# The last contraction chunk of a down projection: 96 rows packed into one full product and two half-array products

## The reference

```python
def _qlinear(x, q, scale, A, Bm):
    w = (q.astype(jnp.float32) - Q_ZERO) * (scale * Q_STEP)[:, None]
    y = jnp.einsum('bsh,oh->bso', x, w)
    return y + LR_SCALE * (x @ A @ Bm)
g = _qlinear(x, gate_q, gate_scale, gate_A, gate_B)
u = _qlinear(x, up_q, up_scale, up_A, up_B)
h = jax.nn.silu(g) * u
return _qlinear(h, down_q, down_scale, down_A, down_B)
...
x = x + _L0_ffn_ref(_L0_cond_ref(x, ...), ...)
x = x + _L1_ffn_ref(_L1_cond_ref(x, ...), L1_ffn_weight)
```

## Time and profile before

| What | Value |
|---|---|
| Median of 3 timed runs | 375.7 us (375.58 to 376.06) |
| Span of the profiled execution (no other time of it is given) | 375.1 us |
| TensorE busy, products | 365.7 us, 97% of the span |
| VectorE, ScalarE, GpSimd busy | 246.0, 190.5, 93.1 us |
| Mean granted TensorE clock | 0.995 of full speed |
| Share of TensorE in the chain that ended last | 82% |
| Products of the down stages (line 660) | 704, 24% of the chain |

### The profile page before, as it was taken

How to read it: one execution, slowest core, us unless ns; L and a number is a source line. 1 busy time by engine, 2 the same in 40 slices (tenths; PEclk the granted TensorE clock), 3 DMA queues, 4 the chain that set the end, 5 groups by cost and what they waited for, 6 DMA issues and landing times.

```text
span 375.1 us, 5791 instructions
## 1 busy us (share of the span) xinstructions
PE 365.7 (97%) x2208; PEld 302.5 (81%) x2208; DVE 246.0 (66%) x399; ACT 190.5 (51%) x345; POOL 93.1 (25%) x78
## 2 busy tenths in 40 slices
PE   8999999999999999999999999999999999998994
PEld 3777887899888888998888889998888899997331
DVE  3858999727476665263766652547889922588995
ACT  4557698403555554134565550235667511066972
POOL 2101432411133224111323232113223321142030
PEclk9899999999999999999999999999999999999999
DMA  7599676197320000142200000526000199977288
GB/s 218 178 228 367 193 264 215 54 336 154 53 44 0 0 0 3 22 64 42 43 0 2 2 0 2 83 36 160 0 3 1 48 287 268 197 163 180 92 174 276
DMA packets 82475, 41.72 MB, mean 111 GB/s; under 512 B 52416, under 2 KB 72784, under 8 KB 82320
## 3 DMA queue, kind: packets, MB, share of 16 engines
q1 hardware_dynamic: 69072, 37.70, 37.2%
q10 hardware_dynamic: 12624, 1.82, 3.1%
q0 software_dynamic: 752, 1.84, 2.5%
HBM read 26.55 MB, written 14.80 MB: 110 GB/s over the span
## 4 chain that ended last, share of the span: by engine, by line
PE 82%; DVE 7%; ACT 4%; DMA 2%; issue 2%; POOL 0%; DVEq 0%
PE ps L675 34%; PE ps L660 24%; PE ps L608 4%; PE ps L690 4%; PE ps L710 3%; PE ps L868 3%; DMA x_nat<-in_gate_q 2%; PE ps L568 2%; PE ps L666 2%; PE ps L712 2%; ACT mix L937 1%; PE ps L848 1%; DVE a_buf L1423 1%; PE ps L623 1%; ACT h_hi L979 1%
## 5 line engine op out<-in xcount | busy, mean ns | idle before, releaser
L1137 POOL TENSOR_TENSOR h_lo<-a_buf,h_hi 128x512 fp32r<-128x512 f32 (+1 forms) x44 | 57.5, 1307 | 121.6 <-ACT h_hi L979 121.6
L660 PE MATMUL ps<-down_w,h_hi 128*128 128x288 f32 (+1 forms) x352 | 76.2, 297 | 0.4 <-POOL h_lo L1137 0.4
L660 PE MATMUL ps<-down_w,h_lo 128*128 128x288 f32 (+1 forms) x352 | 74.8, 293 | 0.0
L675 PE MATMUL ps<-x_hi,gate_w 128*128 128x512 f32 (+1 forms) x176 | 69.9, 397 | 0.0
L675 PE MATMUL ps<-x_hi,up_w 128*128 128x512 f32 (+1 forms) x176 | 69.7, 396 | 0.2 <-DVE b_buf L1416 0.2
L675 PE MATMUL ps<-x_lo,gate_w 128*128 128x512 f32 (+1 forms) x176 | 69.6, 396 | 0.0
L675 PE MATMUL ps<-x_lo,up_w 128*128 128x512 f32 (+1 forms) x176 | 69.3, 393 | 0.0
L660 PEld LDWEIGHTS ps<-down_w,h_hi 128*128 128x128 f32 (+1 forms) x352 | 57.2, 189 | 1.7 <-POOL h_lo L1137 0.6
L660 PEld LDWEIGHTS ps<-down_w,h_lo 128*128 128x128 f32 (+1 forms) x352 | 56.1, 188 | 0.0
L1423 DVE TENSOR_TENSOR a_buf<-a_buf,b_buf 128x512 f32<-128x512 f32 (+1 forms) x44 | 50.0, 1136 | 8.9 <-ACT a_buf L1043 7.8
L1147 POOL TENSOR_TENSOR x_nat<-y_buf,x_nat 128x512 f32<-128x512 f32 x15 | 20.8, 1385 | 94.8 <-DVE y_buf L1309 94.8
(11 more groups left out here) (194 smaller groups left out, 492.7 us busy)
## 6 DMA issues: line engine op xcount, KB each, us to landing
x_nat<-in_x SPq DMA_DIRECT2D x4, 1024.0 KB, 7.1
out<-x_nat SPq DMA_DIRECT2D x15, 256.0 KB, 4.3
turned<-x_nat SPq DMA_DIRECT2D x12, 256.0 KB, 3.3
x_nat<-in_down_q SPq DMA_DIRECT2D x11, 256.0 KB, 3.4
x_nat<-in_gate_q SPq DMA_DIRECT2D x10, 256.0 KB, 7.4
x_nat<-in_up_q SPq DMA_DIRECT2D x10, 256.0 KB, 7.4
edges<-zeros SPq DMA_DIRECT2D x4, 512.0 KB, 9.3
xt_own<-turned SPq DMA_DIRECT2D x6, 256.0 KB, 3.5
```

Source lines behind the costliest of these rows:

```text
L660: last = mm(ps[:, 4 + 2 * (j % 2) + m, 0:HALF + R], part[0:k, ic, j * P:(j + 1) * P], down_w[0:k, ic, m, :], start=first, stop=end)
L675: last = mm(ps[0:k, bank(ic, 2 * m), :], w[:, H * ic + c * k:H * ic + (c + 1) * k], part[:, c, :], start=c == 0 and part is x1_hi, stop=c ...
L1137: nc.gpsimd.tensor_tensor(h_lo[0:k, ic, :], a_buf[0:k, ic % 2, :], plain(h_hi[0:k, ic, :]), ALU.subtract).then_inc(h_lo_ready, 1)
```

## The change

The 1376 features are regrouped at the end. The last 96 features are split in 64 ("tail") and 32 ("rest"). Of each group of tokens the last chunk was four products of 96 rows. Now it is `down_tail`:

- Two full products of 128 rows with `h_hi`, whose chunk 10 holds the high part of all 96 features in rows 0 to 95 (64 tail, 32 rest), and the low part of the 32 rest features in rows 96 to 127. The weights of these 32 rows are laid out twice, at rows 64 to 95 and 96 to 127.
- Two products of 64 rows with `h_lo`, which hold the low part of the 64 tail features twice: in rows 0 to 63 for m = 0 and in rows 64 to 127 for m = 1. They use the two row halves of the array and go to different banks.

The low part of chunk 10 is made by three instructions and no longer by one: GpSimd writes rows 0 to 63 of `h_lo`, and VectorE (`tail_low`) writes rows 96 to 127 of `h_hi` and rows 64 to 127 of `h_lo`. The semaphore `h_tail_ready` counts the two of VectorE. `down_w` has a twelfth chunk for the half m = 1 at rows 64 to 127, with one more transfer (64 x 256 values) and one more conversion. In tile 0 alone the first group's `down_tail` stands inside the second group, ahead of its chunk 4, and the turn and the low-rank product of the first group stand later (ahead of chunk 7, and after the last full chunk).

```diff
+TAIL = P // 2
+TAIL_AFTER = 4
+TAIL_REST = I - (IC - 1) * P - TAIL
...
-        slots += [("down", ic) for ic in range(IC)]
+        slots += [("down", ic) for ic in range(IC)] + [("tail", IC)]
...
-            sp.wait_ge(q_ready, 3 * IC)
+            sp.wait_ge(q_ready, len(slots))
...
+            def down_tail(t, j):
+
+                if j == 0:
+                    pe.wait_ge(h_tail_ready, 2 * t + 1)
+                    if t == 0:
+                        pe.wait_ge(q_ready, len(slots))
+                for m in range(2):
+                    mm(ps[:, 4 + 2 * (j % 2) + m, 0:HALF + R], h_hi[:, IC - 1, j * P:(j + 1) * P],
+                       down_w[:, IC - 1, m, :], start=False, stop=False)
+                if j == 0:
+                    pe.wait_ge(h_lo_ready, (t + 1) * IC)
+                    pe.wait_ge(h_tail_ready, 2 * (t + 1))
+                for m in range(2):
+                    rows = slice(m * TAIL, (m + 1) * TAIL)
+                    last = mm(ps[:, 4 + 2 * (j % 2) + m, 0:HALF + R], h_lo[rows, IC - 1, j * P:(j + 1) * P],
+                              down_w[rows, IC - 1 + m, m, :], start=False, stop=True)
+                last.then_inc(down_mm, 1)
+
+            def tail_later(t, j):
+
+                return t == 0 and j == 0
+
             def down(t, j):
 
+                turn_at, low_rank_at = (0 if mixed_between(t, j) else 4), 8
+                if j > 0 and tail_later(t, j - 1):
+                    turn_at, low_rank_at = 7, IC - 1
...
+                    if j > 0 and ic == TAIL_AFTER and tail_later(t, j - 1):
+                        down_tail(t, j - 1)
+                    if j > 0 and ic == turn_at:
+                        down_turn(t, j - 1)
+                    if j > 0 and ic == low_rank_at:
+                        down_low_rank(t, j - 1)
+                    if ic == IC - 1:
+                        break
...
+                if not tail_later(t, j):
+                    down_tail(t, j)
...
-                    nc.gpsimd.tensor_tensor(h_lo[0:k, ic, :], a_buf[0:k, ic % 2, :], plain(h_hi[0:k, ic, :]),
+                    rows = slice(0, P if ic < IC - 1 else TAIL)
+                    nc.gpsimd.tensor_tensor(h_lo[rows, ic, :], a_buf[rows, ic % 2, :], plain(h_hi[rows, ic, :]),
...
+            def tail_low(t):
+
+                dve.wait_ge(h_hi_ready, (t + 1) * IC)
+                hi = h_hi[:, IC - 1, :]
+                for low, of in ((h_hi[P - TAIL_REST:P, IC - 1, :], slice(TAIL, TAIL + TAIL_REST)),
+                                (h_lo[TAIL:P, IC - 1, :], slice(0, TAIL))):
+                    v.tensor_tensor(low, a_buf[of, (IC - 1) % 2, :], plain(hi[of]),
+                                    ALU.subtract).then_inc(h_tail_ready, 1)
...
                         convert_in_chunk(ic)
+                        convert(len(slots) - 1)
...
+                tail_low(t)
                 for j in range(TG):
                     down_scaled(t, j)
...
+    def by_chunk_and_tail(w):
+
+        w = a(w)
+        rest, tail = w[I - TAIL_REST:], w[I - TAIL_REST - TAIL:I - TAIL_REST]
+        w = np.concatenate([w, rest, np.zeros_like(tail), tail])
+        return w.reshape(IC + 1, P, -1).transpose(1, 0, 2).reshape(P, -1)
```

More of the change, by code:

```diff
@@ L113, in build @@
         x1_lo = sb("x1_lo", [P, HC, TILE], F32R)
-        down_w = sb("down_w", [P, IC, 2, HALF + R], F32R)
+        down_w = sb("down_w", [P, IC + 1, 2, HALF + R], F32R)
         lr_b4 = sb("lr_b4", [P, 2, I], F32R)
@@ L304, in build, with slot_rows @@
         slots = [("gate", ic) if m == 0 else ("up", ic) for ic in range(IC) for m in range(2)]
-        slots += [("down", ic) for ic in range(IC)]
+        slots += [("down", ic) for ic in range(IC)] + [("tail", IC)]
         def slot_width(n):
             kind, ic = slots[n]
-            return H if kind == "down" else HC * width(ic)
+            return {"down": H, "tail": HALF}.get(kind, HC * width(ic))
+        def slot_rows(n):
+            return slice(TAIL, P) if slots[n][0] == "tail" else slice(0, P)
         def slot(n):
-            return x_nat[:, GROUPS - RING + n % RING, 0:slot_width(n)].bitcast(I32)
+            return x_nat[slot_rows(n), GROUPS - RING + n % RING, 0:slot_width(n)].bitcast(I32)
         def slot_values(n):
@@ L318, in slot_dram @@
             kind, ic = slots[n]
-            a = {"gate": gate_q, "up": up_q, "down": down_q}[kind]
-            return a[:, H * ic:H * ic + slot_width(n)]
+            a = {"gate": gate_q, "up": up_q, "down": down_q, "tail": down_q}[kind]
+            first = H * ic + (HALF if kind == "tail" else 0)
+            return a[slot_rows(n), first:first + slot_width(n)]
         def slot_weights(n):
@@ L325, in slot_weights @@
                 return down_w[:, ic, :, 0:HALF]
+            if kind == "tail":
+                return down_w[TAIL:P, ic, 1, 0:HALF]
             w = {"gate": gate_w[:], "up": up_w[:]}[kind]
@@ L494, in _ @@
             sp.dma_start(x_nat[:, TG:2 * TG, :], x_tile(x, 1)).then_inc(x_in[1], 16)
-            for n in range(2 * IC, 3 * IC):
+            for n in range(2 * IC, len(slots)):
                 load_slot(n)
-            sp.wait_ge(q_ready, 3 * IC)
+            sp.wait_ge(q_ready, len(slots))
             for t in range(2, TILES):
@@ L517, in load @@
                     sp.wait_ge(h_lo_ready, TILES * IC)
+                    sp.wait_ge(h_tail_ready, 2 * TILES)
                 if n >= LATE:
@@ L652, in down @@
                             pe.wait_ge(q_ready, 2 * IC + ic + 1)
[L653 to L656, removed]
                     for part in (h_hi, h_lo):
-                        first, end = ic == 0 and part is h_hi, ic == IC - 1 and part is h_lo
                         for m in range(2):
-                            last = mm(ps[:, 4 + 2 * (j % 2) + m, 0:HALF + R], part[0:k, ic, j * P:(j + 1) * P],
-                                      down_w[0:k, ic, m, :], start=first, stop=end)
-                last.then_inc(down_mm, 1)
+                            mm(ps[:, 4 + 2 * (j % 2) + m, 0:HALF + R], part[:, ic, j * P:(j + 1) * P],
+                               down_w[:, ic, m, :], start=ic == 0 and part is h_hi, stop=False)
+                if not tail_later(t, j):
+                    down_tail(t, j)
             def low_rank_a(c, part):
@@ L1608 @@
         "lr_b": np.stack([a(w).reshape(P, LRC) for w in (L0_ffn_gate_B, L0_ffn_up_B)], axis=1).reshape(P, -1),
-        "down_q": by_chunk(a(L0_ffn_down_q)[order].T), "down_s": broadcast(a(L0_ffn_down_scale)[order], P),
-        "down_a": by_chunk(L0_ffn_down_A), "down_b": np.tile(a(L0_ffn_down_B)[:, order], (4, 1)),
+        "down_q": by_chunk_and_tail(a(L0_ffn_down_q)[order].T), "down_s": broadcast(a(L0_ffn_down_scale)[order], P),
+        "down_a": by_chunk_and_tail(L0_ffn_down_A), "down_b": np.tile(a(L0_ffn_down_B)[:, order], (4, 1)),
         "conv_w": conv_w.reshape(P, -1), "ctx_w": a(L1_cond_c_weight).T,
```

6 lines of the change are left out of this document (2 added, 4 removed).

## The result

The changed kernel takes 382.8 us (median of 4 runs, 381.36 to 384.11) against 375.7 for the kernel before: a ratio of 1.0188 [1.0168, 1.0208]. It is slower, as forecast, but by 7.1 us where +3.2 was forecast, and 382.8 is outside the range of 375.3 to 381.0.

What follows compares the result with a forecast made beforehand. It took TensorE's own product pitch as the bound (97% busy); +0.04, +1.9 and +1.3 summed to +3.2 on a 375.1 us span, 378.3, plus 0.6: 378.9 us. Its 8-in-10 range was 375.3 to 381.0.

Steps and rivals of the forecast that it cites:

- Tile 0, first two groups: Tile 0's down stage: the 0.54 stall goes, two tails and a new wait before the third group eat it: +0.04 us.
- 11 plain tails: Last chunks with no wait to absorb their cost: each +0.117 us, together +1.3 us.
- First group of tiles 1 to 3: New wait for low-part subtractions ahead of the half products: +0.71, +0.71 and +0.49 us, together +1.9.
- E: Cost of going from full products to half ones and back: taken as 0.25 us, between bounds 0.20 and 0.36.
- 8-row product: Small product in the first stage, used as the farther bound on the cost of a shape round trip: 0.36 us.
- The exclusion of VectorE and GpSimd: Subtractions with two SBUF operands do not run side by side; the three low-part ones end at about 150.76 in tile 1.
- What was put at nothing: Extra 64 KB transfer and conversion, late loads of `x`, GpSimd's shorter operand, VectorE work behind `tail_low`: no cost.
- Rival 1: Down-stage tails: dear trip, 0.36 us, +4.7, 380.4; or halves one after the other, 380.8; chance 18%.
- Rivals 2 and 3: 2: trip free, exclusion holds, 375.8 us, 15%. 3: pairs free, low parts ready before 150.10, 373.6 us, 9%.
- rival 4: Tiles 1 to 3: only the exclusion of VectorE and GpSimd fails, +1.7, 377.4 us; chance 5%.
- rival 5: Halves run as full products without change of shape, so only waits count: +2.2, 377.9 us; chance 5%.
- The premise that the time lies 0.6 above the span: Whole kernel: timed runs lie 0.6 us above the span, turning a forecast span of 378.3 into 378.9.

Runs made afterwards that it cites:

- before_64: Kernel before, with the two low products of its last chunk cut from 96 to 64 rows in one row half: 384.97 us, ratio 1.0224; repeated 383.16 us.
- one_sub: Changed kernel with the tail's low products over all 128 rows and VectorE's second subtraction of a tile left out: 376.88 us, ratio 1.0025.
- before_later: Kernel before, with tile 0's first-group last chunk moved ahead of chunk 4, turn ahead of 7, low-rank product ahead of 9: 375.43 us, ratio 0.9983.
- later_10: Kernel before, with tile 0's first-group last chunk moved into the second group and the low-rank product ahead of chunk 10: 375.9 us, ratio 0.9995.
- full_rows: Changed kernel with the tail's two low products run over all 128 rows instead of 64, all else kept: 378.21 us, ratio 1.0049.
- two_trips: Changed kernel with the tail's order full, half, full, half instead of full, full, half, half: 390.9 us, ratio 1.0381.
- look_a: Changed kernel, nothing altered, run once more for a profile of a slower execution: 382.25 us.
- look_b: Changed kernel, nothing altered, run again for a second such profile: 381.51 us.

## Why the prediction was right in sign and wrong in size

By its own terms, in us:

| Term | Forecast | Measured | From |
|---|---|---|---|
| Tile 0, first two groups | +0.04 | +0.18 | first product to third group 12.63 before, 79.35 - 66.64 + 0.10 = 12.81 |
| 11 plain tails | +1.3 | +2.9 | 11 x 0.26 |
| First group of tiles 1 to 3 | +1.9 | +2.5 | end of the high part to the next group: 2.10, 2.10, 2.32 before; 2.99, 2.99, 3.00 after, loads included |
| Rest | none | +0.2 | stretch less the three |
| Sum | +3.2 | +5.7 | stretch |

**The failed step is the size of E.** I bounded it by 0.20 from line 848 and 0.36 from the 8-row product, and took 0.25, "nearer to the first". The tail of tile 0 gives 0.39 and `before_64` 0.41: above both bounds, and next to the one that I had put farther away. Of the 2.5 us that the sum is short, 1.6 are in the plain tails and 0.6 in the first groups of tiles 1 to 3.

The lower bound was also misread. The 1.06 begins at line 848's own first start, so what the change into it costs ahead of that start is left out. The next row of the same trace closes the round:

```profile
359.34 1.13 PE L848 MATMUL ps<-x_nat,diag 128*128 128x512 f32 x2
```

From 356.45 to 359.34 is one full round with both changes, 2.89. Two passes of line 848 are 0.86 of it, and the 32 small products, eight groups of four whose single starts in the trace are 0.216 apart, 1.73. That leaves 0.30 for the trip, not 0.20, so the two places said 0.30 to 0.36. What is still missing against 0.39 can be seen too. In `before_64` a change costs 0.09 ahead of it (0.36 instead of 0.27) and 0.10 behind it, for the uncovered load; over the pair on one half both come together (0.46). At line 848 the first change and the second each cost 0.10 ahead of them and the first 0.10 behind it, but behind the second the small products go on at 0.217 at once, with no uncovered load. Why they need none was not tried. The Trainium skill, "TensorEngine Tiling (Array Packing)", Key Properties, says that a change of mode drains the array. The traces agree with that: `before_64` pays for the change without a wait of any kind, 0.09 and 0.10 at a time. The model of a pack in the Trainium skill, "TensorE: Matmul & The Clock Gate", under "Measured speedup vs the span model", has no term for the change. For what lies between the changes the traces agree with it: the two half products start 0.004 apart (74.424 and 74.428 in tile 0), and with the pair side by side it is 0.33 where it is 0.46 in a row.

**The exclusion of VectorE and GpSimd was right**, in mechanism and order. From the end of the high part to the half products I had 2.55 (150.82 - 148.27, and 303.19 - 300.64), the traces have 150.41 - 147.85 = 2.56 and 306.25 - 303.68 = 2.57. `one_sub` shows that most of the wait goes with VectorE's second subtraction. The sum for these tiles was short behind the wait: 0.13 + 0.13 was put for the halves and the way back, and 0.33 + 0.10 came, 0.17 more each. I had let half of E hide in the wait; only the first change can, 0.09 in a plain tail (0.36 instead of 0.27), since the way back and its load come afterwards.

**Tile 0 was right in kind**, and short by 0.14. The stall of 0.54 is gone, the tail does not wait, and a new wait stands ahead of the third group, for line 1309's successor. `before_later` and `later_10` show both halves: the move is worth 0.54 with 8 products behind the low-rank product, and 0.06 with 4.

**What was put at nothing** was right for what was named: no transfer and no conversion shows up in the chain of the down stages. The rest of 0.2 in the table stands in the last groups of tiles 0 to 2, between the condition products and the last chunk. By single starts, the distance from such a group's first product to its last chunk is 5.51 in the kernel before (90.25 to 95.77) and 5.60 in the changed kernel (89.48 to 95.08), 0.09 longer in each of the three. `full_rows` and `one_sub` have 5.60 as well, so it is no part of the trip. I had not looked there, and the cause stays open.

**The rivals.** Rival 1 (E = 0.36, 380.4) was the nearest, and its E was still short; its other form, halves one after the other, is excluded by 0.33 against 0.46. Rivals 2 and 3 are out by `before_64`, rival 4 by the rows of tile 1, rival 5 by the difference between `full_rows` (+2.40, where it had +2.2) and the changed kernel.

**The premise that the time lies 0.6 above the span** was wrong and did no harm. In every run it is 1.8 (381.36 and 379.6). The profiled execution of the kernel before, whose own time was not given, had a late start, with the same six warm-up products at 2.74; counted from the median, 375.7 + 3.2 gives the same 378.9.

## What to carry to other kernels

Count the changes of array shape before the rows that a packing saves: here a pair on two halves saved 0.13 us and its two changes cost 0.40, so by this estimate it needs at least four pairs in a row between two changes to win (no run tried that). Bound the price of a round trip by a distance that begins ahead of the first change and ends behind the second: measured from line 848's own start it was 0.20, over the full round of the same trace 0.30. And measure a small move between two places of the program that both kernels have: the stretch repeated to 0.1 us where medians moved by 1.4.

## What the runs showed of the hardware

- Going between full products and products of 64 rows costs 0.20 us for each change (`two_trips`, 0.33 instead of 0.133 for a product between two changes): 0.09 ahead of the change and 0.10 behind it, where the next weight load is no longer covered (`before_64`; 0.53 instead of 0.43 for a record of two).
- Products with 96 rows pay no change: the kernel before goes from 128 to 96 rows and back with 0.27 for two at every step.
- A VectorE subtraction of 0.69 us makes a GpSimd one issued 0.04 later last 1.79, where the 96-row one of the kernel before takes 1.29 alone; and VectorE's next one lasts 1.67 instead of 0.69 when it is issued behind GpSimd's. All have two inputs in SBUF. The row of three ends 2.4 us after VectorE's first start (147.88 to 150.27).
- Six warm-up products in front of the program took 2.74 us in one execution of the changed kernel and 1.47 in another (`look_a`, `look_b`). The granted clock of the stretch from 6 to 9 us reads 1.00 in both, so the rows do not say why.
